# The store of an expert pair's results stands nine pairs behind the loads in the load queue, in place of six

## What is computed

```python
probs = softmax(x @ gate_w)                     # 64 experts
topk_w, topk_idx = top_k(probs, 8)              # 8 experts for a token
topk_w = topk_w / sum(topk_w)
for each expert e:                              # 64 experts, hidden width 64
    hdn = silu(x @ gate_e) * (x @ up_e)
    acc += combine[:, e] * (hdn @ down_e)
out = acc + sigmoid(x @ shared_gate) * shared_expert(x)
```

## Time and profile before

| | |
|---|---|
| time, median of 3 runs | 1047.55 us (1044.22 to 1063.66) |
| the profiled execution's own time | 1050.35 us |
| its span | 1048.5 us |
| granted TensorE clock, mean | 0.912 |
| PE busy over the span | 866.6 us (83%) |
| DVE, ACT, POOL busy | 626.3, 521.3, 561.8 us |
| DMA traffic | 138.75 MB, mean 132 GB/s |

### The profile page before, as it was taken

How to read it: one execution, slowest core, us unless ns; L and a number is a source line. 1 busy time by engine, 2 the same in 40 slices (tenths; PEclk the granted TensorE clock), 3 DMA queues, 4 the chain that set the end, 5 groups by cost and what they waited for, 6 DMA issues and landing times. The chain is left out here.

```text
span 1048.5 us, 19989 instructions
## 1 busy us (share of the span) xinstructions
PE 866.6 (83%) x6286; PEld 679.6 (65%) x6317; DVE 626.3 (60%) x1794; ACT 521.3 (50%) x1114; POOL 561.8 (54%) x752
## 2 busy tenths in 40 slices
PE   5988999999999998777687764899977686767888
PEld 3766777777777776555565442699866575656545
DVE  6756787787887778776667446334423323333555
ACT  2425766766766765554454345467533333333312
POOL 3686576577568730026555555639724353532470
PEclk9978999999999999898788885599999989889999
DMA  5201112222221106786554245467656566655640
GB/s 146 63 15 41 50 53 76 76 80 76 75 63 62 46 23 148 233 250 208 155 153 147 77 145 200 140 221 241 208 181 193 179 189 184 186 176 174 211 123 25
DMA packets 125892, 138.75 MB, mean 132 GB/s; under 512 B 25174, under 2 KB 111766, under 8 KB 125790
## 3 DMA queue, kind: packets, MB, share of 16 engines
q1 hardware_dynamic: 114270, 106.01, 34.0%
q0 software_dynamic: 11520, 31.47, 9.7%
HBM read 76.44 MB, written 60.83 MB: 131 GB/s over the span
## 5 line engine op out<-in xcount | busy, mean ns | idle before, releaser
L2610 POOL DMA_INDIRECT got_rows<-ys,slot_idx x120 | 115.1, 959 | 151.9 <-issue 47.3
L1856 POOL DMA_INDIRECT xs<-xrow,slot_idx x120 | 116.2, 968 | 85.8 <-DVE slot_idx L1943 31.0
L964 ACT ACTIVATE probs<-bank 128x512 f32<-128x512 f32 x192 | 113.8, 604 | 85.2 <-PE bank L776 48.1
L1708 ACT ACTIVATE probs<-bank 128x512 f32<-128x512 f32 x128 | 74.4, 596 | 102.2 <-PE bank L1608 44.3
L1541 DVE TENSOR_REDUCE xmax<-bank 128x2 f32<-128x512 f32 x128 | 86.0, 685 | 50.9 <-PE bank L1531 26.5
L774 PE MATMUL bank<-query,keys 128*128 128x256 f32 x256 | 82.5, 346 | 0.5 <-ACT probs L964 0.4
L1608 PE MATMUL bank<-query_x,keys_x 114*128 114x512 f32 x128 | 66.9, 528 | 16.1 <-DMA query_x<-xshift 10.8
L1087 DVE TENSOR_REDUCE blockmax<-bank 128x32 f32<-128x512 f32 x96 | 63.1, 686 | 26.6 <-PE bank L726 25.4
L2518 DVE TENSOR_TENSOR xrow<-owner,bank 128x256 f32<-128x256 f32 x60 | 25.2, 420 | 79.6 <-ACT owner L2477 47.6
L2477 ACT ACTIVATE owner<-bank 128x128 f32<-128x128 f32 (+1 forms) x92 | 28.9, 315 | 84.9 <-PE bank L2397 50.8
L1531 PE MATMUL bank<-keys_x,query_x 112*128 112x256 f32 x256 | 60.8, 326 | 1.8 <-DVE xmax L1541 1.7
(11 more groups left out here) (406 smaller groups left out, 2532.0 us busy)
## 6 DMA issues: line engine op xcount, KB each, us to landing
ys<-y_tile SPq DMA_DIRECT2D x62, 256.0 KB
xs<-zero_b SPq DMA_DIRECT2D x16, 512.0 KB, 3.2
up_res<-in_w_up SPq DMA_DIRECT2D x6, 1280.0 KB
ys<-xn SPq DMA_DIRECT2D x30, 256.0 KB
keys_x<-key_rows_x SPq DMA_DIRECT2D x32, 192.0 KB
ctx_in<-in_ctx SPq DMA_DIRECT2D x32, 128.0 KB, 2.5
key_rows_x<-ctx_hi SPq DMA_DIRECT2D x256, 16.0 KB, 1.5
query_x<-xq_rows_hi SPq DMA_DIRECT2D x64, 64.0 KB
```

Of the source, the lines that this page charges most:

```text
L964: nc.scalar.activation(probs[:, u, :], SCORE[u % 2][:], ACT.Exp, scale=SCALE)\
L1708: nc.scalar.activation(probs4[b % 2][:, u, :], XSCORE[n % 2][:], ACT.Exp, scale=XSCALE)\
L1856: nc.gpsimd.indirect_dma_start(out=xs, out_offset=bass.IndirectOffsetOnAxis(ap=slot_idx[:, r, k:k + 1], axis=0), in_=xrow[r % XROW_RING], ...
L2610: nc.gpsimd.indirect_dma_start(out=got_rows[:, g % GOT_RING, :], out_offset=None, in_=ys[0:T * (E + 8 * r + 8), :], in_offset=bass.Indirec ...
```

## The change

In SP's queue the store of a pair comes after the load of the pair nine further on, not six. The number has a name, and the rest is the same number of stores (92) in the same order; the last nine of them now follow the last load, where the last six did.

```diff
         def sparse_loads(sp):
             rows = xs.rearrange("(e c) d -> c e d", c=CAP)
             outs = ys.rearrange("(q a t) d -> q t a d", a=2, t=T)
+            STORE_LAG = 9
...
                 load(p)
-                if p >= 6:
-                    store(p - 6)
-            for p in range(TILES // 2 - 6, TILES // 2):
+                if p >= STORE_LAG:
+                    store(p - STORE_LAG)
+            for p in range(TILE_PAIRS - STORE_LAG, TILE_PAIRS):
                 store(p)
             for q in range(B // 2):
                 out(q)
```

## The result

The kernel with the stores nine pairs behind takes 1009.11 us (median of 4 runs, 1004.52 to 1012.67) against 1045.88 us before (median of 4, 1038.79 to 1063.66): a ratio of 0.967, 95% interval 0.959 to 0.975. Some executions of a kernel are over 1.5% slower than its fastest, and ratios are of the others alone: here they leave out 1063.66 us before, whereas the medians given would have the ratio 0.965. The profiled execution took 1005.59 us with a span of 1003.8 us, 44.7 us less than the span before.

A forecast was written before the change was run, and what follows sets the result against it. PE was taken as the bound in the first 32 pairs, waits, chiefly for loads, in the later ones. 1050.35 - 32 = 1018.4 us, less 2.8 us for the median, gave 1015.5 us; range 984 to 1046.

The forecast's parts named there:

- What bounds the later pairs: Later pairs: PE waits 49.3 us for loads issued late, because SP stands at a store waiting for its result.
- The waits for loads go: Later pairs: loads gain about two steps, so nearly all 49.3 us of PE's waits for them should go.
- signs of being right: PE's load waits under 10 us, SP waiting for turns, less PE idle in later pairs, first 32 still 2.2 us each.
- signs of being wrong: PE waits for ACT and DVE replacing load waits (wrong size); ACT's copy waiting for `ys` stores (wrong sign).
- What the loop gets back: Later pairs: a share of 0.65 of the 49.3 us of load waits comes back as time, 32 us.
- The walk through one sample: Five load waits in later pairs, 9.57 us: 5.58 us back, 0.58, or 0.65 with half of a doubtful 1.36 us.
- The rival in which the gathers absorb the gain: Later pairs: gathers set the pace, time won is lost at the next; within 2%, chance 0.31 including no effect.
- The clock: Later pairs: PE's clock of 0.91 brings nothing in the forecast; at most 15 us from running at full clock.
- The end: After the last tile: the last nine stores wait for results as six did, POOL and DVE move along; cost 0.
- The stores of the first pairs: First 32 pairs: stores go about 1.2 us later, but the cover holds with 1.8 us to spare; cost 0.
- the whole cover of 4.8 us: First 32 pairs: time from a store's later issue until ACT needs its buffer, against landings of at most 3.0 us.
- the slower rival: First 32 pairs: stores land late, holding ACT's copy; decides from landings of about 9 us; over 2% slower, chance 0.07.

## Why the prediction was right, point by point

*What bounds the later pairs: right.* The loads were late because they stood behind a store that waited for its result. One pair more of distance is enough to show it.

*The waits for loads go: right.* 49.3 us to none. Of the signs of being right all came: the waits at the loads' buffers on SP, less idle time on PE, and 2.19 us a pair in the first ones. But signs of being wrong came too, in small: waits of PE for DVE (16.5 us), and waits of ACT's copy for stores (below). They had been named without a size, so they could not decide.

*What the loop gets back, 32 us: too little by 18.8 us, in two terms.* The loop gave 50.8 us. Of the 49.3 us of waits PE's idle time shows 37.3 us, a share of 0.76 in place of 0.65: 5.3 us. The other 13.5 us are PE's busy time, which the forecast had at nothing (next point). The walk through one sample took some waits for covered by the delayed signals. The delays did stay. One of them in the changed kernel, while a batch's gathers run, in the timelines of ACT, of SP and of PE's turns:

```profile
779.55 0.28 ACT L2478 ACTIVATE owner<-bank 128x128 f32<-128x128 f32 x1 [5.25 <-remote]
```
```profile
774.33 0.38 SPq L2303 DMA_DIRECT2D ys<-xn  x1
781.08 0.85 SPq L2298 DMA_DIRECT2D ctx_in<-xs  x2
```
```profile
773.25 0.60 PE L2377 MATMUL bank<-ident,ctx_in 128*128 128x128 f32 x4
775.88 0.63 PE L2377 MATMUL bank<-ident,ctx_hi 128*128 128x128 f32 x4
...
783.64 1.06 PE L2377 MATMUL bank<-ident,ctx_lo 128*128 128x128 f32 x4
786.56 0.60 PE L2377 MATMUL bank<-ident,x_tile 128*128 128x128 f32 x4
```

A turn comes 7.8 us after the one before. The longest such distance is 8.1 us in the changed kernel and was 8.85 us before, so the delays have not gone; but then the pairs follow each other at 2.4 to 2.9 us here, since their loads are there. Before, a delay held up the result, and with it the store and the load behind it. If the delays and the waits for loads were independent, the distance would be worth the same with gathers and without. In the 54 pairs it is worth 50.8 us with gathers, and without them (3.09 - 2.43) x 54 = 36 us: this fits delays that, with six pairs, set off waits for loads on top of themselves. The two figures are of different chips, and no single run shows the step. The rival in which the gathers absorb the gain falls with this, though the gathers do hold what is left of the excess.

*The clock, 0 in the forecast: too low, but the upper bound of 15 us held.* PE's busy time for the same matmuls fell by 13.5 us, and the clock rose from 0.91 to 0.95. Worked as in the prediction, the clock gives about 7 us: 18% of 220.3 us at a busy share of 0.71 is 28 us of half-clock work, 10% of 169.5 us at 0.85 is 14 us, and half of the difference is saved. What the other half is isn't shown, but something like it appears at an unchanged clock. Without gathers, six and then nine pairs, first to last turn:

```profile
756.80:927.30 170.50, 142.50 (x991) 126.51 (x990) 77.44 (x190) 79.17 (x165) 47.20 (x97) 0.99 0.58 178
```
```profile
757.00:891.90 134.90, 133.29 (x983) 125.00 (x984) 75.85 (x190) 78.24 (x163) 45.49 (x95) 0.99 0.72 222
```

At the same clock of 0.99 the busy time falls by 9.2 us, of which the 8 matmuls fewer are about 1 us: where PE waits less, its records are shorter too. Why, the traces don't show; the ends of PE's matmuls are modelled in them.

*The end, 0: wrong in this execution.* It took 78.0 us in place of 70.2, at a clock of 0.91 in place of 1.00. The step that failed is that POOL's gathers "move along" with the tiles: after the last turn POOL still had 34 gathers to issue in place of 27. It is plainer on the chip where the loop went fastest. There POOL had 51 left with nine throughout and 26 with nine in the early pairs only, and the end took 76.2 us in place of 63.1. PE waited 13.5 us in it for DVE, and DVE 18.1 us for gathers:

```profile
DVE X L2660 <- DMA got_rows<-ys,slot_idx: 18.1, 22, 1.8
```

So part of the loop's gain is given back there: the loop ends sooner than the gathers follow. That this is also the cause of the 7.8 us in the first profile isn't shown; no wait of DVE for a gather stands in its end.

*The stores of the first pairs, 0 with 1.8 us to spare: the cost was right, the cover wasn't.* PE's pace stayed at 2.19 us a pair. But ACT now waits for stores there, where it never did: 2.2 + 1.3 = 3.5 us in 4 waits. The longest, with the store that it waits for (three pairs earlier, the same buffer):

```profile
713.36 0.47 SPq L2303 DMA_DIRECT2D ys<-y_tile  x1
```
```profile
719.56 0.59 ACT L2485 COPY y_tile<-bank 128x512 f32<-128x512 f32 x1 [1.60 <-DMA ys<-y_tile]
```

From that store's issue to the copy are 6.2 us, and 5.2 to 5.4 us in the other three cases. So these landings were longer than the whole cover of 4.8 us, and about twice the 3.0 us at most that the prediction had taken from gathers of the later pairs. The pace held because each wait stood alone (1.6 us at most) and ACT had caught up before PE needed it; a landing of over 5 us for every store would have cost, by the slower rival's own sum. This term came out by luck, not by its working. By the rule of the Trainium skill (DMA: Bandwidth & Descriptors, "Queues, rings and completion order") the prediction had an estimate of 1.1 us more for a store right behind its load. The four landings agree with it in direction and go beyond it by over 1 us; no run separates the load in front from the other traffic. The slower rival was about the same place; it came true at twelve pairs, by the later issue and not by landings of 9 us (3.4 us there).

*A slip in the working.* The turns that begin at 758.0 are those of pairs 37 to 91, not 33 to 91: PE turns a pair five steps ahead of its result, and the slow pace begins with the results of pair 32. The pace before was thus 220.3 / 54 = 4.1 us, not 3.8, which moves the slower rival's threshold up by about half a microsecond of landing and leaves the forecast as it is.

The forecast of 1015.5 us is 6.4 us above the measured 1009.11, and that it is so near is in part luck: 18.8 us too little for the loop and 1.7 us for the earlier start, against 7.8 us for the end and 6.3 us because the profiled execution was 2.8 us above the median of its three runs before, and 3.5 us below the median after.

## What to carry to other kernels

In a queue worked off in order, look at what each instruction waits for and what stands behind it: a load behind a store inherits the wait for the result, however free its buffer is. The distance has a lower end, where a load is issued too late to land before its turn, and an upper end, where the store comes after its buffer is wanted back. Here 7 to 9 pairs are alike on the chips with little disturbance, and 8 and 9 on the others; 6 costs 3 to 5%, and 12 costs more than 6 does. Where a wait follows a disturbance, the disturbance stays when the wait is removed; of 49.3 us of such waits 37.3 us were gained as idle time, and 12 us came back as other waits. And a cover is to be taken from the stage where it has to hold: the landings of the later pairs said 3 us, those of the first pairs were 5 to 6.

## What the runs showed of the hardware

On the chips of the first profiles, PE's signals reach the other engines late while POOL's indirect gathers run. In the case above two engines show it at once. PE's turn of ctx_in is down for 773.25 to 773.85, and SP's load for that buffer, with no other DMA in front of it since 774.71, goes only at 781.08; that is 7.8 us after the turn began, where the load before it went 1.5 us after its own turn. ACT's silu comes at 779.55 after 5.25 us idle, though PE had begun the matmuls that it waits for at 774.77 and gone on to the next turn at 775.88. No buffer of the gathers is in any of these steps. With plain DMAs of the same 128 KB the pace is (883.3 - 757.4) / 52 = 2.4 us a pair, where it is 3.1 us with the indirect form in the first profile. That it is the signal which is late, and not the end of the matmuls, is the likelier reading, but the trace can't prove it, for it models their ends.

And this depends on the chip. On the first chip and on those with the kernel before at 1050 and 1051 us the later pairs are slowed. On the two others (980 and 982 us) the real gathers leave a pace of 2.4 us a pair with nine and 2.6 us with seven, from pair 49 to 91:

```profile
755.90:858.20 102.30, 102.20 (x762) 95.49 (x761) 59.99 (x150) 61.04 (x127) 57.99 (x60) 1.00 0.94 289
```

That row is of nine throughout, with 60 of the gathers in it: PE busy 102.20 of 102.30 us, 289 GB/s with the DMA engines 0.94 busy, and no delay. Over half of the 65 to 70 us between the chips lies ahead of the expert stage: pair 0 is turned at 637.8 us there, at 675.3 us in the first profile of the changed kernel. POOL's indirect scatters lie in that part. Why the chips differ is open.
